# Attention: scores of a head's second item moved between the values batches

## What is computed

```python
q = (x @ Wq).reshape(h, n, d); k = (x @ Wk).reshape(h, n, d); v = (x @ Wv).reshape(h, n, d)
a = jnp.einsum('hnd,hmd->hnm', q, k) * scale
a = a + spatial_encoding + edge_encoding        # both are adj
mask = spatial_encoding == 0.0
a = jnp.where(mask, -1000000.0, a)
a = jax.nn.softmax(a, axis=-1)
a = jnp.where(mask, 0.0, a)
out = jnp.einsum('hnm,hmd->hnd', a, v)
return out.transpose(1, 0, 2).reshape(n, h * d) @ Wout
```

## Time and profile before

| what | value |
|---|---|
| median of 3 runs | 3735.41 us (3734.49 to 3735.55) |
| the profiled execution's own time | 3734.03 us |
| its span | 3732.2 us, 58601 instructions |
| PE busy | 2939.7 us, 79% of the span |
| DVE busy | 2372.3 us, 64% |
| ACT busy | 1250.2 us, 33% |
| mean granted clock of PE | 0.919 of full speed |

### The profile page before, as it was taken

How to read it: one execution, slowest core, us unless ns; L and a number is a source line. 1 busy time by engine, 2 the same in 40 slices (tenths; PEclk the granted TensorE clock), 3 DMA queues, 4 the chain that set the end, 5 groups by cost and what they waited for, 6 DMA issues and landing times. The chain is left out here.

```text
span 3732.2 us, 58601 instructions
## 1 busy us (share of the span) xinstructions
PE 2939.7 (79%) x20312; PEld 2136.5 (57%) x20312; DVE 2372.3 (64%) x4629; ACT 1250.2 (33%) x1684; POOL 63.4 (2%) x76
## 2 busy tenths in 40 slices
PE   1449999999999999999995668857775776851868
PEld 1236676767667676766763346645453655641757
DVE  7975555565555555555554798896879877856130
ACT  3433434434334344434442223323143343311020
POOL 0000000000000000000000000000000000003000
PEclk9969999999999999999997789978887888976989
DMA  5755848476584848658484111010110101000415
GB/s 189 294 220 134 199 99 201 112 186 160 138 200 102 196 107 195 152 146 200 95 201 104 40 46 38 31 35 1 35 42 1 35 12 46 24 4 28 147 61 179
DMA packets 587058, 413.70 MB, mean 111 GB/s; under 512 B 538291, under 2 KB 550838, under 8 KB 559030
## 3 DMA queue, kind: packets, MB, share of 16 engines
q1 hardware_dynamic: 584918, 397.51, 39.7%
q10 hardware_dynamic: 2016, 14.68, 1.0%
HBM read 240.10 MB, written 37.81 MB: 74 GB/s over the span
## 5 line engine op out<-in xcount | busy, mean ns | idle before, releaser
L672 DVE SCALAR_TENSOR_TENSOR e_lo<-e,e_hi 128x2048 f16<-128x2048 f32 x128 | 293.3, 2291 | 456.8 <-ACT e_hi L600 456.8
L554 PE MATMUL av<-vw_hi,pT_hi 128*128 128x256 f16 x2048 | 559.9, 273 | 7.5 <-DMA pT_lo<-e_lo 7.5
L554 PE MATMUL av<-vw_lo,pT_hi 128*128 128x256 f16 x2048 | 559.9, 273 | 0.0
L554 PE MATMUL av<-vw_hi,pT_lo 128*128 128x256 f16 x2048 | 559.9, 273 | 0.0
L543 PE MATMUL logits<-kT_hi,qT_hi 128*128 128x512 f16 x1024 | 389.7, 381 | 7.2 <-DVE att_small L658 5.5
L1565 DVE SCALAR_TENSOR_TENSOR nuc_junk<-nuc_e,nuc_thr 128x2048 bf16<-128x2048 f32 x168 | 388.4, 2348 | 5.8 <-issue 1.3
L543 PE MATMUL logits<-kT_lo,qT_hi 128*128 128x512 f16 x1024 | 388.7, 380 | 0.0
L543 PE MATMUL logits<-kT_hi,qT_lo 128*128 128x512 f16 x1024 | 388.7, 380 | 0.0
L594 ACT ACTIVATE att_small<-att_small,minus 128x1 f32<-128x1 f32 x128 | 37.7, 294 | 828.6 <-DVE att_small L667 828.6
L595 ACT ACTIVATE e<-e,att_small,sc 128x2048 f32<-128x2048 f32 x128 | 266.1, 2079 | 0.0
L600 ACT ACTIVATE e_hi<-e 128x2048 f16<-128x2048 f32 x128 | 244.6, 1911 | 15.3
(11 more groups left out here) (410 smaller groups left out, 5985.7 us busy)
## 6 DMA issues: line engine op xcount, KB each, us to landing
bias<-bias_scratch SPq DMA_DIRECT2D x130, 1028.0 KB, 4.8
bias_scratch<-adj_bias SPq DMA_DIRECT2D x16, 1028.0 KB, 3.9
adjT_scratch<-adjT SPq DMA_DIRECT2D x16, 1024.0 KB, 6.9
nuc_at_hi<-adjT_scratch SPq DMA_DIRECT2D x32, 512.0 KB, 3.9
nuc_at_lo<-adjT_scratch SPq DMA_DIRECT2D x32, 512.0 KB, 4.8
l2d_at<-adjT_scratch SPq DMA_DIRECT2D x16, 1024.0 KB, 4.8
l3d_at<-adjT_scratch SPq DMA_DIRECT2D x16, 1024.0 KB, 4.9
adj_rows<-in_adj_dram ACTq DMA_DIRECT2D x14, 1024.0 KB, 8.6
```

The source lines that it names most:

```text
L554: last = nc.tensor.matmul(AV[par][:, :], PT[par][w][:, m, :], VW[x][:, m, :], start=(m == 0 and w == x == 0), stop=(m == T - 1 and w == 1))
L672: nc.vector.scalar_tensor_tensor(out=EL[:, :], in0=E[par][:, :], scalar=P_SCALE, in1=EH[:, :], op0=ALU.mult, op1=ALU.subtract).then_inc(lo ...
```

## The change

`project` keeps only the three projections K, Q and V. The fourth projection and the `qk` of a head's second item (item 1) become one function, `values_and_qk`. It issues the 8 values batches in order, and behind every second batch one quarter of the scores of item 1: 6 matmuls of 512 columns, one bank of one half of the logits. Behind the first four batches come the two quarters of half 0, behind the other four those of half 1. `scores` is incremented at the end of each half, as before. The loop over `u` was a loop of the engine with a register; here it is unrolled in Python, so the addresses are constants. Nothing changes on ACT, DVE and SP.

```diff
--- before.py
+++ after.py
@@ -503,30 +503,16 @@
                     with pe.Fori(0, 2) as u:
                         if n == 0:
                             pe.wait_ge(logits_read, 32 * h + READS_FREE)
-                        if n == 3:
-                            pe.wait_ge(wo_hi_s, h + 1)
-                            pe.wait_ge(wo_lo_s, h + 2)
                         for b in range(4):
-                            if kind is None:
-                                pe.wait_ge(vw_free, PER_VW * h + 4 * u + b + 1)
-                                if b == 0:
-                                    pe.wait_ge(bank_free, KQV * (h + 1) + BANKS_FREE)
-                                for m in range(2):
-                                    o = VP[b % 2][:, m * D:(m + 1) * D]
-                                    for k in range(KC):
-                                        for w, x in ((0, 0), (0, 1), (1, 0)):
-                                            last = nc.tensor.matmul(o, VT[w][:, k, ds((4 * u + b) * 2 * P + m * P, P)], WO[x][:, k, :],
-                                                                    start=(k == 0 and w == x == 0), stop=(k == 1 and w == 1))
-                            else:
-                                pe.wait_ge(bank_free, KQV * h + 8 * n + 4 * u + b + 1)
-                                for m in range(2):
-                                    o = bank[b][:, m * ROWS:(m + 1) * ROWS]
-                                    for k in range(KC):
-                                        for w, x in ((0, 0), (0, 1), (1, 0)):
-                                            W = (WH, WL)[w][kind[0]]
-                                            hT = (hT_hi, hT_lo)[x]
-                                            last = nc.tensor.matmul(o, W[:, k, ds((4 * u + b) * D + m * P, P)], hT[:, k, ds(h * ROWS, ROWS)],
-                                                                    start=(k == 0 and w == x == 0), stop=(k == 1 and w == 1))
+                            pe.wait_ge(bank_free, KQV * h + 8 * n + 4 * u + b + 1)
+                            for m in range(2):
+                                o = bank[b][:, m * ROWS:(m + 1) * ROWS]
+                                for k in range(KC):
+                                    for w, x in ((0, 0), (0, 1), (1, 0)):
+                                        W = (WH, WL)[w][kind[0]]
+                                        hT = (hT_hi, hT_lo)[x]
+                                        last = nc.tensor.matmul(o, W[:, k, ds((4 * u + b) * D + m * P, P)], hT[:, k, ds(h * ROWS, ROWS)],
+                                                                start=(k == 0 and w == x == 0), stop=(k == 1 and w == 1))
                             last.then_inc(proj, 1)
 
                 def qk(i, t, first=None):
@@ -544,6 +530,34 @@
                                                             start=(k == 0 and w == x == 0), stop=(k == 1 and w == 1))
                         last.then_inc(scores, 1)
 
+                def values_and_qk(h, i, t):
+
+                    for u in range(2):
+                        if u == 0:
+                            pe.wait_ge(wo_hi_s, h + 1)
+                            pe.wait_ge(wo_lo_s, h + 2)
+                            pe.wait_ge(bank_free, KQV * (h + 1) + BANKS_FREE)
+                        for b in range(4):
+                            pe.wait_ge(vw_free, PER_VW * h + 4 * u + b + 1)
+                            for m in range(2):
+                                o = VP[b % 2][:, m * D:(m + 1) * D]
+                                for k in range(KC):
+                                    for w, x in ((0, 0), (0, 1), (1, 0)):
+                                        last = nc.tensor.matmul(o, VT[w][:, k, (4 * u + b) * 2 * P + m * P:(4 * u + b) * 2 * P + (m + 1) * P],
+                                                                WO[x][:, k, :], start=(k == 0 and w == x == 0), stop=(k == 1 and w == 1))
+                            last.then_inc(proj, 1)
+                            if b % 2:
+                                if b == 1:
+                                    pe.wait_ge(logits_read, 2 * i + u + READS_FREE - 1)
+                                c0 = u * 2 * BANK + b // 2 * BANK
+                                for k in range(KC):
+                                    for w, x in ((0, 0), (0, 1), (1, 0)):
+                                        last = nc.tensor.matmul(L[u][:, b // 2 * BANK:(b // 2 + 1) * BANK], QT[w][:, k, t * P:(t + 1) * P],
+                                                                KT[x][:, k, c0:c0 + BANK],
+                                                                start=(k == 0 and w == x == 0), stop=(k == 1 and w == 1))
+                                if b == 3:
+                                    last.then_inc(scores, 1)
+
                 def av(i, par, h):
                     pe.wait_ge(vw_free, PER_VW * (h + 1) + VW_FREE)
                     pe.wait_ge(av_free, i + 1)
@@ -566,8 +580,7 @@
                 for n in range(3):
                     project(0, n)
                 qk(0, 0, 0)
-                project(0, 3)
-                qk(1, 1)
+                values_and_qk(0, 1, 1)
                 with pe.Fori(0, HEADS - 1) as h:
                     items(h)
                     for n in range(3):
@@ -575,8 +588,7 @@
                     av(T * h + T - 2, 0, h)
                     qk(T * h + T, 0, h + 1)
                     av(T * h + T - 1, 1, h)
-                    project(h + 1, 3)
-                    qk(T * h + T + 1, 1)
+                    values_and_qk(h + 1, T * h + T + 1, 1)
                 items(HEADS - 1)
                 av(T * HEADS - 2, 0, HEADS - 1)
                 av(T * HEADS - 1, 1, HEADS - 1)
```

## The result

The changed kernel takes 3748.01 us (median of 7 runs, 3744.58 to 3749.35) against 3735.41 us before (7 runs, 3733.48 to 3735.96). The ratio is 1.0034, with a 95% interval of 1.0022 to 1.0045: slower by 12.6 us. Timed a second time beside other kernels it took 3749.57 us against 3735.40, ratio 1.0040 (1.0026 to 1.0055). Forecast was 3750.3, in 3747.5 to 3755.

A forecast was written before the change was run, and what follows sets the result against it. The prediction took the ACT and DVE ring to set the pace, with DVE's in-order queue behind the last values batch deciding each boundary. Seven heads' 13.6 us plus 1.3 for the first gave +14.9, so 3750.3 us, range 3747.5 to 3755.

The forecast's parts named there:

- The removal: PE's values block at each head: all three stalls on the values evacuation go, 1.95 us of PE's time per head.
- The net shift of the last batch: Head boundary: three quarters move the last values batch 3.89 us later, filled stalls 1.95 earlier; net +1.94 per head.
- No give-back in the loop: Items behind a head's boundary: no gap returns the delay; loop items stay 10.5 us apart.
- the ACT and DVE ring: Inside a head: ACT and DVE wait for each other, 10.52 us per item, setting the pace; PE runs 0.1 below.
- Head 0: First head's boundary: first quarter goes into PE's existing stop; +1.3 us if the clock falls again, -0.2 if not.
- The prediction's other case: First head, shorter stop leaves the clock up: batches three to eight take 10.4 us, shift -0.2 us.
- The sum: Whole kernel: 13.6 us from seven heads plus 1.3 from the first, +14.9 us.
- the later stages: Stages whose clock comes and goes: range widened a little below, from the forecast's own bound of 3748.8 to 3747.5 us.
- A: Rival at the head boundary: the fill pays, PE keeps its 1.95 us in seven heads, 3721.8 us; chance 0.04.
- B: Rival in the loop: hidden slack returns 1.4 to 1.7 of the 1.94 us per head, about 3739; chance 0.05.
- C: Rival at every boundary: PE's clock falls and visibly costs 7 x 1.7 = 12 us more, 3762; chance 0.06.
- the prediction's signs: Trace in attention: PE's values-evacuation waits fall from 24 to about one; its read wait grows to about 4.7 us per head.

The follow-up runs named there:

- e1: The change with the old order on PE: unrolled, but all four quarters behind the eight values batches; 3732.03 us, ratio to before 0.9989.
- e2: The change with only one quarter ahead, between values batches 2 and 3, the other three behind batch 8; 3738.64 us, ratio to before 1.0009.
- e3: The change with all four quarters ahead of the last two values batches, DVE's order as before; 3760.46 us, ratio to before 1.0067.
- e5: The change with DVE reading both halves of item 1's logits behind the last values evacuation, item 0's rest after them; 3746.16 us, ratio to before 1.0028.
- e4: The change plus 40 spare 256-column matmuls behind its block, results unused, filling most of PE's stop; 3748.80 us, ratio to before 1.0038.
- e9: Old PE order, unrolled, without quarters ahead; DVE makes item 0's rest between the sixth and seventh values evacuations; 3728.83 us, ratio to before 0.9980.
- e6: The change with DVE reading half 0 of item 1's logits behind the fourth values evacuation; 3740.34 us, ratio to before 1.0015.
- e7: Against before: all four quarters ahead of the last two batches, DVE's item 0 rest and item 1 reads between evacuations; 3707.68 us, ratio 0.9928.
- e10: The change with DVE making item 0's rest behind the second values evacuation, both item 1 reads behind the eighth; 3731.01 us, ratio to before 0.9988.

## Why the prediction was right

**The removal.** All three stalls per head are gone, as forecast, 1.95 us of PE's time. The prediction gave the unroll nothing further; e1 shows that 0.31 of the 1.95 was the unroll's.

**The net shift of the last batch.** Forecast +1.94 us per head; L679 is +1.95 from V0, item 0 to item 1 +1.95 (23.48 to 25.43). e2 and e3 move it by the number of quarters ahead, less the stalls that these fill.

**No give-back in the loop.** From item 1 to item 15 it takes 147.58 us for 147.59. The forecast that the ACT and DVE ring sets the pace held in each variant except e5, which put a second wait into the ring.

**Head 0.** Forecast +1.3 with the clock falling, -0.2 without. It fell: V2 was released after 3.56 us idle, the granted clock was 1.00 for the first microsecond and 0.50 over 303.8 to 307.0 by the stretch below, and item 0 to item 1 took 25.32 for 23.97, +1.35. The prediction's other case adds up to 10.46 us and -0.1, not 10.4 and -0.2.

```profile
302.64 0.28 PE L546 MATMUL vw_ps<-wo_hi,vT_hi 128*128 128x256 f16 x1 [3.56 <-DVE vw_lo L704]
```

```profile
303.80:307.00 3.20, 3.20 (x16) 2.18 (x15) 0.69 (x1) 0.60 (x1) 0.00 (x0) 0.50 0.52 96
```

**The sum.** 14.9 forecast, 14.8 in the profiled attention; 12.6 and 14.2 between medians. In the trace, the 2 us that the first comparison shows less lie behind attention, in code that the change doesn't touch. That the median, 3748.01, still fell into the range was partly luck: it is 0.5 us above the lower end of 3747.5, the prediction allowed 1.3 us for the later stages, and their time alone differs by up to 10 us between the traces of all kernels.

**The rivals.** A (the fill pays) fell with the result, and e3 against the change shows why: the later the last batch, the slower. B (slack in the ring) fell to the 147.58. C was right that the clock would fall at every boundary, and wrong in its cost, as e4 shows. Of the prediction's signs, PE's waits on `vw_lo` fell as said, and its wait on the read grew to 4.6 us by its rows, 4.7 counted from start to start as the prediction does.

**Not settled:** why the code behind attention takes between 1724 and 1734 us in the traces. DVE's busy time in it is the same (1183.1 us in the trace of before, 1183.4 in e9's, which took 1734.3), so it waits longer. Half of the 7.6 us between these two lies in two waits for PE in a later layer (the diffusion), where DVE takes a row maximum. DVE's timelines of before:

```profile
2277.50 2.29 DVE L1562 TENSOR_REDUCE nuc_nmax<-nuc_l 128x1 f32<-128x2048 f32 x1 [4.15 <-PE nuc_l L1311]
...
2397.59 2.29 DVE L1562 TENSOR_REDUCE nuc_nmax<-nuc_l 128x1 f32<-128x2048 f32 x1 [4.47 <-PE nuc_l L1311]
```

and of e9:

```profile
2267.74 2.29 DVE L1597 TENSOR_REDUCE nuc_nmax<-nuc_l 128x1 f32<-128x2048 f32 x1 [6.08 <-PE nuc_l L1346]
...
2390.45 2.29 DVE L1597 TENSOR_REDUCE nuc_nmax<-nuc_l 128x1 f32<-128x2048 f32 x1 [6.19 <-PE nuc_l L1346]
```

These waits are short in the traces of before, e1, e3, e4 and both of the change, and 1.5 to 2.1 us longer each in e2, e5, e6, e7, e9 and e10. So the medians of the latter may hold some microseconds that have nothing to do with attention; what makes PE late there was not followed. Against before, attention alone is 30.7 us shorter in e7's trace, 12.0 in e9's and 9.9 in e10's.

## What to carry to other kernels

A stall on the busiest engine is worth filling only with work that nobody downstream is waiting behind: count by how much the last instruction of the interleaved block moves (here three quarters of 1.30 us against 1.95 us of stalls), and look at what is queued behind it on the next engine. If that engine takes its list in order, reorder it together with the first: here quarters between the batches cost 12.6 us alone (25 with all four ahead of the last two batches), and gained 28 us with all four ahead and DVE's rest and reads moved into the idle time that opens. With that list the last batch stands late and costs little: for item 1, only the exponential is left behind it.

Before work is moved behind other work, ask which single buffer it fills: item 0's rest, put behind two reads, tied the ring to a transpose.

## What the runs showed of the hardware

In every head of the change and of e3, PE's stop of 4.5 to 5.9 us behind the block went with a granted clock of 0.50 for 3.4 to 6.8 us, which began behind the stop or already in it. The stop of 0.7 us (before, e1) was followed by none, the one of 2.0 us in e2 by one in three heads of seven, and the one of 2.9 to 3.0 us in e5 (before `av`) by one in five of seven. In the first head the clock fell also after the shorter stop of 3.6 us before V2, which the forecast had left open. At the later heads, where the ring of ACT and DVE sets the pace, the half clock cost nothing (e4).

PE left its waits for `vw_lo` 0.1 us sooner when the batches were unrolled and the weight loads behind the wait had constant addresses: 0.35 us idle in e1 for 0.46 before, three times per head.
